# A 32-image gating and Fourier-mixing block on one core: the spatial product stays pixel-major and is transformed onto VectorE's terms in PSUM

## What is computed

```python
x = x + _L0_conv_ref(_gn(x), ...)            # channel gate
# _L1_conv_ref on _gn(x), B=32, 128 channels, MED=256, NF=4
r = relu(conv1x1(x)); r = relu(conv1x1(r)); r = conv1x1(r)
routeing = softmax(r.mean(axis=(2, 3)).reshape(Bn, NF, MED), axis=1)
s = relu(conv3x3(x)); s = conv3x3(s)
spatial_routeing = softmax(s.mean(axis=(2, 3)).reshape(Bn, NF, MED), axis=1)
xp = jnp.einsum('bhwc,mc->bhwm', xc, w_pw1)
xp = star_scale * jnp.square(jax.nn.relu(xp)) + star_bias
xf = jnp.fft.rfft2(xp, axes=(1, 2), norm='ortho')
weight = jnp.einsum('bfc,hwf->bhwc', routeing, cw)
spatial_weight = jnp.einsum('bfc,hwf->bhwc', spatial_routeing, spatial_weights)
xs = jnp.fft.irfft2(xf * weight, s=(H, W), axes=(1, 2), norm='ortho')
out = xp * spatial_weight + xs
out = jnp.einsum('bhwm,dm->bhwd', out, w_pw2)
```

## Time and profile before

| | |
|---|---|
| time, median of 3 runs | 259.8 us (259.14 to 264.2) |
| profiled execution, first to last instruction | span 257.2 us; no time of its own is given beside it |
| median less span | 2.6 us |
| busy: PE, DVE, ACT, POOL | 240.7, 194.2, 161.1, 108.9 us |
| granted TensorE clock | 1.000 of full speed |

### The profile page before, as it was taken

One profiled execution on the slowest core, in us unless ns is written; L12 is line 12 of the kernel. 1 busy time (PEld: TensorE's weight loads), 2 busy tenths in 40 slices (PEclk: granted clock), 3 DMA queues, 4 the chain that ended last, 5 costly groups with the idle time before them and its releaser, 6 DMA issues.

```text
span 257.2 us, 6874 instructions
## 1 busy us (share of the span) xinstructions
PE 240.7 (94%) x2225; PEld 187.7 (73%) x2225; DVE 194.2 (76%) x548; ACT 161.1 (63%) x380; POOL 108.9 (42%) x197
## 2 busy tenths in 40 slices
PE   0697799999999999999999999999999999999995
PEld 0686765554545555886988889988888888888984
DVE  3988999955939626996779998858767768768773
ACT  2034586645976748755676677676676676676772
POOL 2422440120000002257455665765665665665663
PEclk9999999999999999999999999999999999999999
DMA  7999200000000000001010010010010010010002
GB/s 212 364 326 348 105 3 3 1 4 3 0 3 0 3 0 0 4 23 35 9 43 20 23 42 24 20 43 20 20 43 20 20 41 20 20 41 20 23 20 82
DMA packets 9483, 13.19 MB, mean 51 GB/s; under 512 B 732, under 2 KB 8924, under 8 KB 9332
## 3 DMA queue, kind: packets, MB, share of 16 engines
q1 hardware_dynamic: 9428, 12.80, 15.3%
q10 hardware_dynamic: 32, 0.08, 0.2%
HBM read 8.69 MB, written 4.19 MB: 50 GB/s over the span
## 4 chain that ended last, share of the span: by engine, by line
PE 70%; DVE 11%; issue 8%; POOL 4%; DMA 3%; ACT 2%; SPq 1%; POOLq 0%; DVEq 0%; ACTq 0%
PE bank L1198 19%; PE bank L1359 10%; PE bank L1305 8%; PE bank L1371 8%; PE bank L1292 6%; PE bank L1106 4%; PE bank L1378 4%; PE bank L1334 3%; DMA x_all<-in_x 3%; PE bank L1136 1%; POOL prod L421 1%; PE bank L1263 1%; PE bank L1213 1%; PE bank L1348 1%; DVE stats L726 1%
## 5 line engine op out<-in xcount | busy, mean ns | idle before, releaser
L420 POOL TENSOR_TENSOR prod<-t_re,t_im 128x256 f32<-128x256 f32 x31 | 22.6, 729 | 51.6 <-DVE t_re L1007 51.2
L988 DVE TENSOR_SCALAR xp<-sq_v,later_sb 128x512 f32<-128x512 f32 x32 | 17.6, 550 | 32.2 <-ACT sq_v L588 31.9
L1198 PE MATMUL bank<-z_all,split_h 128*64 128x450 f16 (+2 forms) x320 | 37.4, 374 | 1.0 <-ACT z_all L503 1.0
L1359 PE MATMUL bank<-later_sb,prod 128*128 128x128 f32 x256 | 36.3, 285 | 0.2 <-POOL prod L421 0.2
L430 POOL TENSOR_TENSOR waves<-folded 128x128 f32<-128x128 f32 x31 | 14.1, 455 | 51.1 <-DVE eo L995 47.4
L1305 PE MATMUL bank<-later_sb,eo 128*128 128x128 f32 x256 | 34.2, 276 | 0.4 <-DVE eo L994 0.4
L1359 PEld LDWEIGHTS bank<-later_sb,prod 128*128 128x128 f32 x256 | 31.1, 192 | 3.9 <-POOL prod L421 2.3
L1305 PEld LDWEIGHTS bank<-later_sb,eo 128*128 128x128 f32 x256 | 31.1, 192 | 1.5 <-DVE eo L994 0.7
L1371 PE MATMUL bank<-qt,later_sb 128*128 128x256 f32 x124 | 31.9, 380 | 0.0
L618 ACT ACTIVATE folded<-bank,coef 128x128 f32<-128x128 f32 x31 | 11.4, 367 | 32.5 <-PE bank L1378 26.2
L1198 PEld LDWEIGHTS bank<-z_all,split_h 128*64 128x64 f16 x320 | 17.2, 110 | 16.0 <-issue 3.1
(11 more groups left out here) (176 smaller groups left out, 495.2 us busy)
## 6 DMA issues: line engine op xcount, KB each, us to landing
x_all<-in_x SPq DMA_DIRECT2D x8, 512.0 KB, 8.6
out<-x_all SPq DMA_DIRECT2D x32, 128.0 KB, 1.7
sp_t<-in_branch_s SPq DMA_DIRECT2D x1, 2560.0 KB, 15.6
later_sb<-in_later SPq DMA_DIRECT2D x1, 918.5 KB, 8.8
sym_all<-in_sym SPq DMA_DIRECT2D x1, 292.5 KB
early_sb<-in_early SPq DMA_DIRECT2D x1, 278.0 KB, 3.6
rwf_t<-in_branch_r SPq DMA_DIRECT2D x1, 256.0 KB, 11.8
kan_sb<-in_kan ACTq DMA_DIRECT2D x1, 80.8 KB, 3.3
```

The lines of the kernel that those rows point to most:

```text
L420: pool.tensor_tensor(prod[:, :, :, 0, :], halved[0][:, :, 0], halved[1][:, :, 1], ALU.subtract).then_inc(prod_ready, 1)
L1198: last = mm(dst[:, :, rows_out, cols_out], w[:, t, :], pixels(z_all[:, b:b + 2, part, :])[:, :, rows_in, cols_in], start=(n == 0 and t in ...
L1359: last = mm(bank[1][:, odd * C:(odd + 1) * C], prod[:, m, odd].rearrange("p a s -> p (a s)"), pw2_t[:, m, :], start=(m == 0), stop=(m == 1))
```

## The change

The spatial product is no longer turned to channel-major and taken through `pw2` by itself. It stays pixel-major, and because the transform is linear, its own forward transform is added to the real-and-imaginary terms in front of the reduction, so reduction and inverse transform serve both. In detail:

- DVE computes the spatial product `qt` from `xp` and the pixel mix, which now comes out pixel-major in bank 4 (no `swt` copy on ACT). POOL folds it into even and odd sums (`fold`), and PE transforms these (`waves_onto`) with accumulation onto `total` in bank 5, where DVE has just written the frequency terms. For this a matmul of 512 columns and 32 rows (`primed`) is issued ahead, in `mix`; what it writes is overwritten.
- The pixel transposes, the `qt` matmuls through `pw2` and the sum in bank 6 go. `products` moves from POOL to DVE and reads bank 5; `odd_sum` moves from DVE to POOL; the last addition to `x_all` moves from POOL to DVE.
- The square of ACT writes `xp` directly: the root of the scale's size is folded into the relu's scale, its sign into the filters, the bias into the even sum and the spatial product as a scalar.
- `expand` runs three images ahead instead of two. The last image's own path goes. POOL's wait on the DVE sums goes.

The core of the diff:

```diff
-            def products(i):
-                pool.wait_ge(terms_ready, 3 * i + 3)
+            def odd_sum(i, p):
+                pool.wait_ge(sq_ready, i + 1)
...
+                pool.tensor_tensor(eo[p][:, 1, :], xp[p][:, 0, :], xp[p][:, 1, :], ALU.subtract).then_inc(odd_ready, 1)
+
+            def fold(i):
+                pool.wait_ge(qt_ready, i + 1)
...
+                pool.tensor_tensor(qt_eo[:, 0, :], qt[:, 0, :], qt[:, 1, :], ALU.add).then_inc(q_folded, 1)
+                pool.tensor_tensor(qt_eo[:, 1, :], qt[:, 0, :], qt[:, 1, :], ALU.subtract).then_inc(q_folded, 1)
...
-                if ahead:
-                    pool.wait_ge(eo_ready, 2 * i + 8)
...
-            def halves(i, p):
+            def even_sum(i, p):
...
+                dve.scalar_tensor_tensor(out=eo[p][:, 0, :], in0=xp[p][:, 0, :], scalar=shift_2[:, 0:1], in1=xp[p][:, 1, :],
+                                         op0=ALU.add, op1=ALU.add).then_inc(even_ready, 1)
+
+            def spatial(i, p):
+                dve.wait_ge(pixel_done, i + 1)
...
+                dve.scalar_tensor_tensor(out=qt[:, :, :], in0=xp[p], scalar=shift[:, 0:1], in1=mixed_pixel,
+                                         op0=ALU.add, op1=ALU.mult).then_inc(qt_ready, 1)
...
+                tt(total[:, :, :, 2:P], spec[:, :, :, 2:P], mixed_slot[:, :, 0, 2:P].unsqueeze(2).broadcast_to(wide_shape), ALU.mult).then_inc(re_ready, 1)
...
+            def products(i):
+                dve.wait_ge(q_done, i + 1)
...
+                halved = [t.rearrange("p m a (o s) -> p m a o s", o=2) for t in (total, t_im[:, :, :, :])]
+                tt(prod[:, :, :, 0, :], halved[0][:, :, 0], halved[1][:, :, 1], ALU.subtract).then_inc(prod_ready, 1)
+                tt(prod[:, :, :, 1, :], halved[0][:, :, 1], halved[1][:, :, 0], ALU.add).then_inc(prod_ready, 1)
...
+            def round_of(i, p, between=None):
+                products(i)
+                even_sum(i + 2, p)
+                spatial(i + 1, 1 - p)
+                if between:
+                    between()
+                terms(i + 1)
+                if not isinstance(i, int) or i >= 1:
+                    finish(i - 1)
...
+            def waves_onto(i):
+
+                pe.wait_ge(re_ready, 2 * i + 2)
+                for odd in range(2):
+                    pe.wait_ge(q_folded, 2 * i + 1 + odd)
+                    for m in range(2):
+                        last = mm(total[:, m, :, 64 * odd:64 * odd + 64], qt_eo[:, odd, m * P:(m + 1) * P], forward[:, odd, :, :],
+                                  start=False, stop=(odd == 1 and m == 1))
+                last.then_inc(q_done, 1)
...
+                    if not isinstance(i, int) or i >= 1:
+                        pe.wait_ge(prod_ready, 2 * i)
+                    else:
+                        pe.wait_ge(r2_ready, 2 * NIT)
+                    spare = slice(BLOCK * (2 - 2 * j), BLOCK * (3 - 2 * j))
+                    mm(bank[5], ident_b[spare, :], filters[spare, :], start=True, stop=False).then_inc(primed, 1)
...
-                for m in range(2):
-                    last = mm(bank[6][:, 0:HW], pw2_t[:, m, :], qt[:, m, :], start=(m == 0), stop=(m == 1))
-                last.then_inc(sp_done, 1)
```

More of the change, by code:

```diff
@@ L431, in unfold @@
                 pool.tensor_tensor(waves[:, 1, :], folded[:, 0, :], folded[:, 1, :], ALU.subtract).then_inc(waves_ready, 1)
[L432 to L439, removed]
-            unfold(0)
[L441 to L450, removed]
+            odd_sum(0, 0)
+            odd_sum(1, 1)
+            fold(0)
+            fold(1)
+            odd_sum(2, 0)
+            unfold(0)
+            fold(2)
+            odd_sum(3, 1)
+            with pool.Fori(1, NB // 2 - 1) as j:
+                for p in range(2):
+                    unfold(2 * j + p - 1)
+                    fold(2 * j + p + 1)
+                    odd_sum(2 * j + p + 2, p)
+            unfold(NB - 3)
+            fold(NB - 1)
+            unfold(NB - 2)
         @block.scalar
@@ L484, in _ @@
             act.wait_ge(filt_done, 1)
-            act.activation(f_res[:, 0:2, :], bank[5][:, 0:2 * NF].rearrange("p (a f) -> p a f", a=2), ACT.Identity).then_inc(filt_copied, 1)
+            act.wait_ge(sign_set, 1)
+            act.activation(f_res[:, 0:2, :], bank[5][:, 0:2 * NF].rearrange("p (a f) -> p a f", a=2), ACT.Identity,
+                           scale=sign[:, 0:1]).then_inc(filt_copied, 1)
             sigmoid_sum(0, 0)
@@ L494, in _ @@
             sigmoid_sum(0, 1)
-            ahead(ACT.Sqrt)
+            act.wait_ge(sign_set, 2)
+            act.activation(root[:, :], size[:, :], ACT.Sqrt).then_inc(root_set, 1)
             deviation(0, 2)
@@ L918, in _ @@
             z_low(4)
+            star_scale()
             edges(0, 4)
@@ L1048, in _ @@
             round_of(3, 1)
-            halves(6, 0)
-            logits(1)
-            terms(5)
-            spatial(5)
-            finish(4)
+            round_of(4, 0, lambda: logits(1))
             centred(1)
@@ L1320, in transform @@
-            def transform(i, p):
-                waves_of(i, p)
-                turn_pixels(i, p)
-            def mix(i, pair, j):
-                pe.wait_ge(rt_out, pair + 1)
-                if not isinstance(i, int) or i >= 1:
-                    pe.wait_ge(terms_ready, 3 * i)
-                    pe.wait_ge(sw_ready, i)
-                for m in range(2):
-                    for s in range(2):
-                        start = BLOCK * (2 * j + s)
-                        last = mm(bank[3 + s][:, m * HW:(m + 1) * HW], route[start:start + BLOCK, m, :],
-                                  filters[start:start + BLOCK, (1 - s) * HW:(2 - s) * HW], start=True, stop=True)
-                last.then_inc(w_done, 1)
+            def waves_onto(i):
[6 more added lines that the diff above has]
+                last.then_inc(q_done, 1)
@@ L1398, in _ @@
             expand(1)
+            mix(0, 0, 0, (0,))
             taps(7, 2, 5)
```

345 lines of the change are left out of this document (154 added, 191 removed).

## The result

The changed kernel takes 266.25 us (median of 4 runs, 266.08 to 267.69), the kernel before in the same comparison 260.06: a ratio of 1.027 (95% interval 1.022 to 1.031), slower. The forecast was 258.2 us, 1.6 us less than before; the kernel became 6.2 us slower, near the upper end of the stated range. The profiled executions have spans of 264.3 and 257.2 us, 7.1 apart.

The account below looks back on a forecast made before the run. PE's matmuls were taken to bound the kernel. From the profiled 257.2 us: -7.8 (28 rounds, 4.81 to 4.53), +1.0 start, +3.1 middle, +2.1 end gave 255.6; plus 2.6 for the median, 258.2 us, range 252.5 to 267.

Parts of the forecast that it names:

- What a round loses and gains on PE: PE's steady round: from 4.70 to 4.40 us without a route turn, from 4.91 to 4.61 with one.
- the priming matmul takes a third block, so it can be free ... I take 0.05: Added 512-column PE matmul before the mix: runs beside the mix's row blocks, 0.05 us charged, 0.21 if alone.
- that is +0.06: PE's wait before the mix for DVE's products: 0.23 us where 0.17 stood, per round.
- About 0.9 us of room: DVE in a steady round: work on the loop ends near 3.6, leaving about 0.9 us for anything else.
- the hold: DVE's even sum or finish held up by POOL: up to 0.47 us, charged at 0.03 a round.
- The ring: One image's loop PE, DVE, PE, DVE, POOL, PE before the next enters bank 5: 4.32 us, under PE's 4.40.
- The middle, 3.1: Second half's routing on DVE between rounds: losses of 1.1, 0.8 and 1.2 us, against almost nothing before.
- The start, 1.0: From the last hidden activation to the third image's forward transform: 106.4 against 105.43 us, +1.0.
- The end, 2.1: From image 29's added transform to the last sum: 13.8 us against 11.7, +2.1.
- Faster: Rival, 17%: PE runs at bare work, rounds of 4.29 and 4.50, half of what is given back hides: 251.4 us.
- Priming not hidden: Rival, 15%: the priming matmul on PE costs 0.21 us instead of 0.05, period 4.69: 262.6 us.
- Slower: Rival, 16%: the loop through bank 5 bounds, DVE's even sum held by POOL's unfold, round 4.9: 268.5 us.

Follow-up runs that it names:

- e5: Changed kernel with bank 6 instead of 5 for odd images from 7 on and for images 1 and 3: 260.03 us, 0.9995 of the kernel before.
- e11: Changed kernel with an unneeded DVE memset of 128x1024 per round in rounds 14 to 29: 269.56 us, a single run.
- e9: e5 with the last addition to x_all back on POOL, ACT scaling x_all first: 258.23 us, 0.993 of the kernel before.
- e1: Kernel before without the second half's routing (images 16 to 31 take that of images 0 to 15): 255.56 us, 0.984 of the kernel before.
- e7: Changed kernel with the priming matmul issued twice: 270.57 us, 1.039 of the kernel before.
- e4: Changed kernel with bank 6 instead of bank 5 for odd images from 7 on, priming matmul kept: 261.73 us, 1.007 of the kernel before.
- e2: Changed kernel without the second half's routing (images 16 to 31 take that of images 0 to 15): 257.73 us, 0.989 of the kernel before.
- e8: Changed kernel with an unneeded DVE memset of 128x512 per round in rounds 14 to 29: 265.76 us, 2 runs.
- e12: Kernel before with an unneeded DVE memset of 128x1024 per round in rounds 14 to 29: 265.29 us, a single time.
- e10: e9 with DVE's routing work cut up and spread over rounds 0 to 12, logits read at the end of round 4: 255.82 us, 0.982 of the kernel before.
- e3: Changed kernel with the same DVE routing work cut into pieces and spread over rounds 0 to 13: 271.53 us, 1.041 of the kernel before.
- e6: e5 with the second half's window and image sums on POOL instead of DVE: 260.83 us, 1.003 of the kernel before.

## Why the prediction was wrong, step by step

The stages of my sum run from the forward transform of image 2 (105.43 before, 107.50 after) to that of image 30 (243.32 and 248.20) and on to the last sum. Measured: start +2.07, 28 rounds +2.81 (of which 28 x -0.10 = -2.8 steady and +5.6 routing stage), end +1.95, and 0.3 outside; 7.1 in all, for -7.8 + 1.0 + 3.1 + 2.1 = -1.6.

- **"What a round loses and gains on PE": the bare work was right.** e5 runs at 4.40 and 4.67, for 4.40 and 4.61. DVE's products, which now read the bank, take 0.42 and 0.41, as taken. The step that failed is "the priming matmul takes a third block, so it can be free ... I take 0.05", together with "that is +0.06" for the wait. Free it is, in e5. But in the changed kernel it waits for the products and so sits ahead of the mix: the mix starts 0.10 behind it, and is 0.10 longer. The sum had taken the wait and the matmul as two small terms and missed that the one undoes the other's cover. By the stage from mix 10 to 30 the shared bank costs 3.05 us in 20 rounds (94.04 less 90.99), 0.15 each. This is most of the 5.0 us by which the term -7.8 was too good.
- **"About 0.9 us of room": too large.** e11 gives 0.64 and 0.86. The finish, for which I had charged no hold because it had "0.9 us of room", lasts 0.63, where it takes 0.47 beside an idle POOL (the last one, at 258.43). POOL's odd sum beside it takes 0.89 where the earlier trace rows gave 0.73 for that shape:

```profile
L1036 DVE SCALAR_TENSOR_TENSOR x_all<-x_all,coef,waves 128x256 f32 (+1 forms) x31 | 19.6, 631 | 0.0
...
L430 POOL TENSOR_TENSOR eo<-xp 128x256 f32<-128x256 f32 x32 | 28.4, 888 | 44.2 <-ACT xp L607 44.2
```

  In e9, where the finish is not on DVE, the odd sum takes 0.73 and the even sum 0.62 instead of 0.52: the hold moves on (the even sum takes 0.47 to 0.48 in the rounds where POOL is idle beside it, 0.54 to 0.77 in those where it meets both of POOL's unfold additions), and costs nothing there: mix 10 to mix 30 takes 90.82 us, 90.99 in e5. In the changed kernel the finish and the odd sum are each longer by 0.16 beside the other, not by the other's whole length.
- **The middle, 3.1: measured 5.6.** The right kind of loss, in the right place. Set against the kernel before round by round, with the steady 0.10 left out, two parts stand in no term: `windows` (mix 1 to 2, 5.58 us) with 0.8, and `routing_part`, up to 1.44 us of DVE work each (147.47 to 148.91; mix 8 to 10, 5.35 and 5.56), with 1.5; together 2.3. What was in the sum was too small: image sums 1.5 for 1.1, logits and centring 1.4 for 1.2, softmax 1.0 for 0.8. Against it stand 0.7 us that the kernel before loses behind its own image sums and the changed one does not (mix 3 to 4, 5.53 and 4.76). So "against almost nothing now" was wrong as well: the kernel before takes 46.67 us from mix 1 to mix 10 and 43.01 without its routing (e1).
- **The start, 1.0: measured 2.07.** The chain left out the added transform of image 1, 0.90, which stands between the inverse of image 0 and the forward transform of image 2. The rest came as added up, to 0.2.
- **The end, 2.1: measured 1.95, by two errors that cancel.** 13.8 was counted from the added transform of image 29, 0.89 ahead of the point from which 11.7 was counted, so the chain gave +1.2. The ring is 4.62 there (mix 30 to mix 31), not 4.32.
- **The rivals.** "Faster" needed rounds of 4.29 and 4.50; even with two banks (e5) they are 4.40 and 4.67. "Priming not hidden" had a mean round of 4.69, and the changed kernel's is 4.70, but not because the matmul runs alone for its 0.21: e5 hides it whole, and a second one costs 0.09 (e7). "Slower" had the right sign and, with 268.5, nearly the time, but by the hold on the even sum, and that is luck: in the steady rounds the even sum takes 0.47 to 0.48, and over all rounds 0.52. What decided was a bank shared by two images, and DVE work inside the loop. The ring was in the forecast, computed at 4.32 against PE's 4.40, and taken as covered. A margin of 0.08 us on a sum of a dozen terms is no cover: the term that was at stake was the wait between products and mix.

What is shown by a run: the bank (e4, e5), the routing work (e1, e2), the room (e8, e11, e12), the price of a second priming matmul (e7), the work per round (e9, e10). The start and the end are read from the trace and were not tried apart.

## What to carry to other kernels

When a change takes an engine that ran ahead and puts it into the loop of the engine that bounds, count its side work in full: measure its room with a dummy instruction before and after (here at least 1.0 us became 0.64 and 0.86), not its busy share, which hardly moved (81.67 to 86.13 of 105 us). A buffer that two successive items share is a wait even where everything "just fits"; try a second one first (here it was worth 6.2 us of 266). Spreading helped where rounds had been relieved first (e10) and not where they hadn't (e3).

## What the runs showed of the hardware

- An idle stretch of PE can be followed by a stretch at the lower clock, and so cost more than itself. In e2 the two idle stretches of 0.93 and 0.94 us around 102 are followed by 3.4 us at the lower of the two levels, 0.50 of full speed; per us from 104, with the granted clock in the last but two column:

```profile
104.00:105.00 1.00, 1.00 (x9) 1.00 (x8) 0.94 (x2) 0.39 (x1) 0.12 (x1) 0.66 0.00 0
105.00:106.00 1.00, 1.00 (x6) 0.89 (x6) 1.00 (x3) 0.00 (x0) 1.00 (x2) 0.50 0.06 16
106.00:107.00 1.00, 1.00 (x7) 0.74 (x5) 0.06 (x1) 0.38 (x1) 0.98 (x2) 0.50 0.00 0
107.00:108.00 1.00, 1.00 (x8) 1.00 (x7) 0.00 (x0) 0.68 (x1) 0.00 (x0) 0.64 0.00 0
```

  From the mix of image 1 to the forward transform of image 2 PE takes 5.21 us there (103.52 to 108.73), and 3.66 in the changed kernel at the full clock (103.95 to 107.61): 1.55 us on top of the 1.9 of idling. The same shows in e4 and e11 at the same place (0.50 for 3.4 us from 104.2 and 104.1 on), in e7 and e6 from 116.7 and 118.5 us on, behind idle stretches of 1.64 and 1.41, and not in the profiled executions of the changed kernel and of e8, whose idle stretches are the same as in e11; so the runs show that it can come, not when.
- Matmuls on different row blocks run beside each other for nothing (the five of a mix with its priming in e5 take 0.32 us, as the four of the kernel before do), but not when the first of them waits for another engine: then the next starts 0.10 to 0.13 later, in nearly all of the changed kernel's mixes and in e5 only in those of images 5 and 6.
- In e3 and e12 the part up to the first mix took 4.4 to 4.5 us longer. The 128x128 matmuls near the start, from 14 to 28 us, in the changed kernel and in e3:

```profile
L1134 PE MATMUL bank<-early_sb 128*128 128x128 f32 x65 | 8.2, 279 | 0.0
L1155 PE MATMUL bank<-early_sb 128*128 128x128 f32 x41 | 10.0, 432 | 0.0
```

  From 10 to 12 us they take 421 and 433 ns, and from 30 us on 282 and 283. The clock column says 1.00 all along, but the trace's first entry for the clock, at the full level, stands at 12.80 us in the changed kernel and at 28.93 in e3 (12.83 in the kernel before, 28.95 in e12). So the clock rose 16 us later in these two executions, and ahead of its first entry the column can't be trusted. Why it rose later no run shows.
